# Output projection of a gated delta-rule block in float32 instead of float16 pairs

## The chip, the cores and the metric

The kernel runs on one core of one Trainium2 chip. The metric is the device time of one execution in microseconds; the median of three runs of the kernel before is 2579.32 us (2579.14 to 2581.09).

## The reference

The input x is 8 sequences of 512 tokens with 256 channels. Three sublayers are added to it in turn:

```
x = x + 0.5 * ffn(layernorm(x))
x = x + attention(layernorm(x))
x = x + 0.5 * ffn(layernorm(x))

attention(x):                      # 16 heads of 128 channels
  q, k, v = silu(conv4(x @ Wq)), silu(conv4(x @ Wk)) / sqrt(128), silu(conv4(x @ Wv))
  alpha, beta = sigmoid(x @ Wa + ba), sigmoid(x @ Wb + bb)
  for each token:  S = alpha * S - beta * (S @ k - v) k^T ;  o = S @ q
  o = layernorm_per_head(o) * ln_w + ln_b
  o = o * sigmoid(x @ Wg)          # the gated rows
  return o @ Wo                    # the output projection: 2048 channels to 256
```

The change is in the last line of the attention. The feed-forward layers use weights rounded to 8-bit floats.

## The kernel before

The program has three phases: the first feed-forward layer, the attention, the second feed-forward layer. The residual stream stays in SBUF throughout.

The attention goes over 4 groups of 4 heads (`HG`, `U`), in each group over the 8 sequences, in each sequence over 4 chunks of 128 tokens: 128 steps. A step works on one chunk of 4 heads. There is no planner: each engine has a hand-written order of stages (its `step(s)`), in which stages of neighbouring chunks are interleaved, and semaphores between them. In step s TensorE (PE) projects chunk s+3, inverts the triangular system of chunks s and s+1 by six levels (`level_a`, `level_b`), updates the state with chunk s-1, and turns and projects the output rows of chunks s-1 and s-2.

Float32 products that should be nearly exact are in places done as three float16 products: each operand is split into a high and a low half, and high*high + low*high + high*low is added up in PSUM. The output projection is one of these places. For chunk t:

- ScalarE (ACT) `affine` (L1221) writes the normed rows, float32, to `oa`; GpSimd (POOL) `gated` (L937) multiplies them with the gate.
- ACT `high` (L1229) writes the float16 high half `oh`; POOL `low` (L944) writes the low half `ol`.
- PE `output` (L1476) does 4 heads x 3 = 12 float16 matmuls, each with a stationary 128x128 tile of `oh` or `ol` and 256 moving columns of `wo16`.
- VectorE (DVE) `output` (L1060) adds the PSUM result, divided by 64, to the stream.

PE calls `output(s - 2)` in step s just before `level_b(s, 5)`, whose result ACT is waiting for.

The projection weights of a group are loaded in jobs (`load_job`, L1564 and L1567, on the SP queue) through four `raw` buffers; ACT (L1587, L1589) multiplies by 64 and writes the high half, POOL (L1597) the low half. A group has 16 jobs for Wk, Wq, Wv, Wg and 4 for Wo. For groups 1 to 3 they are done in the last steps of the group before (`JOB_STEPS`): the Wo jobs all in one step, on ACT and POOL in the same step in which PE first needs the new `wo16` (single-buffered, so no earlier). Group 0's jobs are spread over the first feed-forward layer.

Of the kernel before, what the change touches and what calls it, by code (L numbers as in the profile page):

```python
# [8 lines left out]
F16 = mybir.dt.float16  # L9
# [22 lines left out]
CX = C + 1  # L32
JOBS = 4 * U + U
SLOTS = 4
WO_SLOTS = 1
JOB_STEPS = {0: (0, 1, 2), 1: (3, 4, 5), 2: (6, 7, 8), 3: (9, 10, 11), 4: (12, 13, 14), 5: (15,), 8: (16, 17, 18, 19)}
FIRST_JOB_STEP = -26
# [22 lines left out]
def ffn_phase(nc, first, x_in, y_out, stream, z16, kit, scratch, w):  # L60

    with ExitStack() as ctx:  # L62
# [84 lines left out]
        def _(sp):  # L147
# [26 lines left out]
            if first:  # L174
# [556 lines left out]
def attention_phase(nc, stream, z16, kit, scratch, w):  # L731

    with ExitStack() as ctx:
# [9 lines left out]
        def units(b):  # L743
# [4 lines left out]
        nhalf, epsd, minus, lnb, lnwn = (kit[k] for k in ("nhalf", "epsd", "minus", "lnb", "lnwn"))  # L748
        bcol, prm, kqv16, gate16, wo16 = (kit[k] for k in ("bcol", "prm", "kqv16", "gate16", "wo16"))

# [13 lines left out]
        on = sb("on", [P, U, D]); oa = sb("oa", [P, U, C])  # L764
        oh = sb("oh", [P, U, C], F16); ol = sb("ol", [P, U, C], F16)

# [4 lines left out]
            dve="scan at mix y0 y1 res w z bn mv out " + " ".join(f"{k}{j}" for k in ("tap", "conv") for j in range(U)),  # L771
            act="rhs16 w16 kdec t0 lev0 lev1 on oa oh "
                + " ".join(f"{k}{j}" for k in ("acc", "silu", "gate") for j in range(U)),
            pool="diag am tt al kg qg zs var rstd shift og ol",
        )
# [29 lines left out]
        def _(sp):  # L805
# [28 lines left out]
        def _(pool):  # L834
# [104 lines left out]

            def low(t):  # L940
                if not known(t):
                    return
# [8 lines left out]
            def step(s):  # L951
                root(s - 1)
                low(s - 2)
                system_low(s + 1)
# [14 lines left out]
        def _(dve):  # L969
# [144 lines left out]
        def _(act):  # L1114
# [101 lines left out]
            def affine(t):  # L1216
                if not known(t):
                    return
                act.wait_ge(m["pe_ot"], t + 1)
                need(act, m["pool_ol"], t)  # L1220
                nc.scalar.activation(oa[:, :, :], units(TURN), ACT.Identity, bias=lnb[:, :], scale=lnwn[:, :])\  # L1221
                    .then_inc(m["act_oa"], 1)

            def high(t):
                if not known(t):
                    return
                act.wait_ge(m["pool_og"], t + 1)
                need(act, m["pe_wo"], t)
                nc.scalar.activation(oh[:, :, :], oa[:, :, :], ACT.Copy).then_inc(m["act_oh"], 1)  # L1229

            def weights(s):
                for job in jobs_of(s):
                    group, x = divmod(job, JOBS)
                    if x < 4 * U:
                        need(act, m[f"pe_pj{x % U}"], NC * (B * group - 1) + x // U + 1)
                    else:
                        need(act, m["pe_wo"], NC * B * (group - WO_SLOTS + 1))
                    high_job(nc, kit, act, job)

            def step(s):  # L1240
# [12 lines left out]
                first_inverse(s + 1)  # L1253
                high(s - 2)
                acc(s + 3, 1)
# [17 lines left out]
        def _(pe):  # L1273
# [5 lines left out]
            def gram_k(t):  # L1279
# [7 lines left out]
                if t > 2:  # L1287
                    pe.wait_ge(m["act_oa"], t - 2)
                else:
                    need(pe, m["dve_mix"], t)  # L1290
                    need(pe, m["act_kdec"], nk(t))
                cols = slice(c * C, (c + 1) * C)
# [4 lines left out]
            def gram_q(t):  # L1297
# [7 lines left out]
                pe.wait_ge(m["dve_at"], t + 1)  # L1305
                cols = slice(c * C, (c + 1) * C)
# [4 lines left out]
            def k_turned(t):  # L1311
                if not known(t) or t % NC == NC - 1:
                    return
                n, c = divmod(t, NC)
                pe.wait_ge(m["dve_mix"], t + 1)
                for u in range(U):
# [64 lines left out]
            def first_solution(t):  # L1381
# [4 lines left out]
                pe.wait_ge(m[f"act_lev{par}"], NL * (t // 2 + 1))  # L1386
                if t > 1:
                    pe.wait_ge(m["dve_out"], t - 1)
                else:
                    need(pe, m["dve_w"], t)  # L1390
                    need(pe, m["dve_z"], nk(t))
                for u in range(U):
# [53 lines left out]
            def out_turned(t):  # L1446
# [3 lines left out]
                if known(t + 2) and (t + 2) % NC < NC - 1:  # L1450
                    pe.wait_ge(m["act_kdec"], nk(t + 2) + 1)
                elif known(t + 2):
                    pe.wait_ge(m["dve_mix"], t + 3)
                else:
                    pe.wait_ge(m["act_oa"], t)
                for u in range(U):
# [3 lines left out]
            def output(t):  # L1460
# [4 lines left out]
                if n % B == 0 and c == 0:  # L1465
                    pe.wait_ge(kit["pool_wl"], JOBS * (group + 1))
                pe.wait_ge(m["pool_ol"], t + 1)
                if known(t + 1) and (t + 1) % NC < NC - 1:
                    pe.wait_ge(m["dve_z"], nk(t + 1) + 1)
                elif known(t + 1):  # L1470
                    pe.wait_ge(m["dve_w"], t + 2)
                else:
                    pe.wait_ge(m["dve_out"], t)
# [81 lines left out]
def load_job(nc, kit, w, sp, job):  # L1555
# [5 lines left out]
    need(sp, kit["pool_wl"], job - SLOTS + 1)  # L1561
    if x < 4 * U:
        src = w[("Wk", "Wq", "Wv", "Wg")[x // U]].rearrange("(k p) (h d) -> h p k d", p=P, d=D)[h]
        sp.dma_start(kit["raw"][:, slot].rearrange("p (k d) -> p k d", k=KT), src).then_inc(kit[f"dma_w{slot}"], 16)  # L1564
    else:
        src = w["Wo"].rearrange("(h p) n -> h p n", p=P)[h]
        sp.dma_start(kit["raw"][:, slot], src).then_inc(kit[f"dma_w{slot}"], 16)  # L1567


def split_of(kit, job, which):  # L1570
# [3 lines left out]
    if i < 3:  # L1574
        return kit["kqv16"][:, which, i, j].rearrange("p k d -> p (k d)")
    if i == 3:
        return kit["gate16"][:, which, j].rearrange("p k d -> p (k d)")
    return kit["wo16"][:, group % WO_SLOTS, which, j]

# [21 lines left out]
def macaron(nc, names, aps, out):  # L1601
# [5 lines left out]
    with ExitStack() as ctx:  # L1607
        stream = ctx.enter_context(nc.sbuf_tensor("stream", [P, B, TT, H], F32))
        with ExitStack() as inner:
            def sb(name, shape, dt=F32):  # L1610
# [9 lines left out]
                raw=sb("raw", [P, SLOTS, H]), kqv16=sb("kqv16", [P, 2, 3, U, KT, D], F16),  # L1620
                gate16=sb("gate16", [P, 2, U, KT, D], F16), wo16=sb("wo16", [P, WO_SLOTS, 2, U, H], F16))
            for k in [f"dma_w{i}" for i in range(SLOTS)] + ["act_w64", "act_wh", "pool_wl"]:
                kit[k] = inner.enter_context(nc.semaphore("k_" + k))
# [25 lines left out]
```

## Time and profile before

| | |
|---|---|
| median of 3 runs | 2579.32 us |
| profiled execution, its own time | 2582.29 us |
| its span | 2580.1 us |
| mean granted TensorE clock | 0.978 |
| PE busy | 2401.2 us, 93% |
| ACT / DVE / POOL busy | 78% / 77% / 64% |

The table is from one profiled execution; its span runs from the first to the last instruction. PE is TensorE's matmuls, PEld its weight loads, which run beside them. Matmuls are pipelined: one takes longer from its start to its end than the distance to the next one's start, and the distance is what it costs. So costs are read as (start of the next group - start of this group) / count. A float32 matmul is two matmul instructions in the trace (four heads of 128x128 stand there as x8), a float32 transpose one.

### The profile page before, as it was taken

Reading aid. Unit: us, or ns where it says so; the run is one execution under the profiler, and the core shown is the slowest. Engines: PE = TensorE matmul, PEld = TensorE weight load, DVE = VectorE, ACT = ScalarE, POOL = GpSimd, SP = SyncE. Lnnn points to the kernel's source line nnn. Section 1 sums busy time; section 2 is a strip of 40 time slices with the busy share of each in tenths; the row PEclk is TensorE's granted clock in tenths of the full one; section 3 lists DMA queues with packets and bytes.
Section 4 is the critical chain, followed back from the end, with each engine's and each line's share of the span. In section 5 each row is a group of like instructions: output and inputs, shape, how many; then the busy total and the mean of one; then the engine's idle time right before and its main releaser. Section 6 shows DMA issues by size and latency. Waiting matters only on the chain. (4 is left out here: it accounts for less than half of the span.)

```text
span 2580.1 us, 64359 instructions
## 1 busy us (share of the span) xinstructions
PE 2401.2 (93%) x24496; PEld 1838.1 (71%) x24496; DVE 1993.1 (77%) x4217; ACT 2018.4 (78%) x3848; POOL 1659.0 (64%) x1929
## 2 busy tenths in 40 slices
PE   4996899999999999999999999999999999999598
PEld 2553677777777777777777777777777777777365
DVE  5555888888878788888788888888778888887254
ACT  2884788888888788888887888888888888887364
POOL 7662566666677666666676666667766666666365
PEclk8998999999999999999999999999999999999799
DMA  5000111111121011111111111111111111111001
GB/s 137 22 14 8 34 30 28 27 29 31 36 55 40 23 30 30 30 31 30 47 42 38 31 30 31 29 27 40 50 38 30 29 27 28 29 31 28 23 26 41
DMA packets 80610, 87.86 MB, mean 34 GB/s; under 512 B 21937, under 2 KB 50609, under 8 KB 80177
## 3 DMA queue, kind: packets, MB, share of 16 engines
q1 hardware_dynamic: 80304, 83.75, 12.5%
q8 instruction: 196, 3.21, 0.5%
q14 instruction: 110, 0.89, 0.1%
HBM read 77.83 MB, written 5.90 MB: 32 GB/s over the span
## 5 line engine op out<-in xcount | busy, mean ns | idle before, releaser
L1496 PE MATMUL a_bank<-k_z,k_kqv 128*128 128x512 f16 x2304 | 588.8, 380 | 11.9 <-DVE a_kb L1073 5.9
L1187 ACT ACTIVATE a_inv<-a_bank 128x512 f16<-128x512 f32 x640 | 383.8, 605 | 123.2 <-PE a_bank L1354 122.8
L1004 DVE TENSOR_TENSOR k_y<-a_bank,k_masks 128x256 f16<-128x256 f32 x768 | 320.0, 420 | 176.8 <-PE a_bank L1340 169.1
L937 POOL TENSOR_TENSOR a_oa<-a_oa,a_gb 128x512 f32<-128x512 f32 x128 | 163.2, 1275 | 303.4 <-ACT a_oa L1221 303.4
L859 POOL TENSOR_TENSOR a_am<-a_at,k_ident 128x512 f16<-128x512 f32 x128 | 162.9, 1273 | 241.1 <-DVE a_at L989 241.1
L1496 PEld LDWEIGHTS a_bank<-k_z,k_kqv 128*128 128x128 f16 x2304 | 200.9, 98 | 155.4 <-issue 17.8
L1340 PEld LDWEIGHTS a_bank<-a_inv,a_am 128*128 128x128 f16 x3072 | 164.8, 98 | 198.3 <-ACT a_inv L1187 80.9
L1073 DVE SCALAR_TENSOR_TENSOR a_kb<-a_bank,k_prm,a_kb 128x511 f32<-128x511 f32 (+2 forms) x384 | 281.0, 739 | 19.1 <-ACT a_kb L1131 15.2
L1073 DVE SCALAR_TENSOR_TENSOR a_vb<-a_bank,k_prm,a_vb 128x511 f32<-128x511 f32 (+2 forms) x384 | 280.9, 739 | 2.2 <-ACT a_vb L1131 0.6
L1073 DVE SCALAR_TENSOR_TENSOR a_qb<-a_bank,k_prm,a_qb 128x511 f32<-128x511 f32 (+2 forms) x384 | 280.6, 738 | 1.8 <-ACT a_qb L1131 1.5
L1354 PE MATMUL a_bank<-a_inv,k_y 128*128 128x64 f16 x3072 | 273.2, 193 | 0.4 <-DVE k_y L1004 0.4
L1340 PE MATMUL a_bank<-a_inv,a_am 128*128 128x64 f16 x3072 | 202.1, 194 | 53.6 <-ACT a_inv L1187 39.2
L1352 PE MATMUL a_bank<-k_y,a_inv 128*128 128x64 f16 x2560 | 237.5, 193 | 3.0 <-DVE k_y L1004 3.0
L1354 PEld LDWEIGHTS a_bank<-a_inv,k_y 128*128 128x128 f16 x3072 | 208.9, 98 | 20.3 <-DVE k_y L1004 0.5
L1352 PEld LDWEIGHTS a_bank<-k_y,a_inv 128*128 128x128 f16 x2560 | 199.6, 98 | 28.5 <-DVE k_y L1004 14.2
L1476 PE MATMUL a_bank<-k_wo,a_oh 128*128 128x256 f16 x1024 | 193.8, 277 | 20.8 <-POOL k_wo L1597 11.4
L1212 ACT ACTIVATE a_on<-a_bank,a_shift,a_rstd 128x128 f32<-128x128 f32 x512 | 193.0, 468 | 8.3 <-POOL a_shift L927 8.3
L1496 PE MATMUL a_bank<-k_z,k_gate 128*128 128x512 f16 x768 | 197.8, 382 | 0.3 <-DVE a_vb L1073 0.3
L1442 PE MATMUL a_bank<-a_wv,a_mix 128*128 128x128 f32 x1024 | 193.5, 281 | 0.2 <-DVE a_wv L1023 0.2
L905 POOL TENSOR_TENSOR a_qg<-a_qb,a_cum 128x512 f32<-128x512 f32 x96 | 113.1, 1178 | 96.1 <-PE a_bank L1442 96.1
L1441 PE MATMUL a_bank<-a_z,a_qg 128*128 128x128 f32 x768 | 164.7, 296 | 1.6 <-DVE a_wv L1023 1.6
L980 DVE TENSOR_TENSOR_SCAN a_prod<-a_decay,k_diag 128x516 f32<-128x516 f32 x128 | 157.9, 1233 | 1.1 <-ACT a_kdec L1162 1.1
(151 smaller groups left out, 6831.1 us busy)
## 6 DMA issues: line engine op xcount, KB each, us to landing
a_decay<-decay_rows SPq DMA_DIRECT2D x128, 258.0 KB, 3.3
a_cum<-cumulative_rows SPq DMA_DIRECT2D x96, 258.0 KB, 3.3
stream<-in_L_attn_x SPq DMA_DIRECT2D x8, 512.0 KB, 6.8
out<-stream SPq DMA_DIRECT2D x8, 512.0 KB, 2.9
k_raw<-in_L_attn_Wk SPq DMA_DIRECT2D x16, 128.0 KB, 3.6
k_raw<-in_L_attn_Wq SPq DMA_DIRECT2D x16, 128.0 KB, 3.4
k_raw<-in_L_attn_Wv SPq DMA_DIRECT2D x16, 128.0 KB, 2.9
k_raw<-in_L_attn_Wg SPq DMA_DIRECT2D x16, 128.0 KB, 3.5
```

Source lines behind the costliest of these rows:

```text
L937: nc.gpsimd.tensor_tensor(oa[:, :, :], oa[:, :, :], gb[:, n % 2, :, c * C:(c + 1) * C], ALU.mult).then_inc(m["pool_og"], 1)
L1004: nc.vector.tensor_tensor(even(y16[:, j], mb), bank[LEV[par]][:, 0:U * C // 2].rearrange("p (u b m) -> p u b m", u=U, m=mb), masks[:, j].r ...
L1073: nc.vector.scalar_tensor_tensor(out=dst[:, d:S], in0=bank[PJ[j % 2]][:, 0:S - d], scalar=prm[:, i, U * (n // B) + j, TAPS - 1 - d:TAPS - ...
L1187: nc.scalar.activation(both, bank[LEV[par]][:, :].rearrange("p (two b m) -> p two b m", two=2, m=mb), ACT.Copy).then_inc(m[f"act_lev{par}" ...
L1212: ins = nc.scalar.activation(on[:, u], bank[OUT][:, u * D:(u + 1) * D], ACT.Identity, bias=shift[:, u:u + 1], scale=rstd[:, u:u + 1])
L1340: mm = pe.matmul(at_half(LEV[par], 0, u), am16[:, par, u], halves(t16[par][:, u], mb, 0), start=True, stop=True)
L1352: pe.matmul(at_half(LEV[par], 0, u), tt16[par][:, u], halves(y16[:, j, u], mb, 0), start=True, stop=True)
L1354: mm = pe.matmul(at_half(LEV[par], half, u), y16[:, j, u], halves(tt16[par][:, u], mb, 1), start=True, stop=True)
L1441: pe.matmul(units(OUT)[:, u], qg[:, u], z[:, u], start=True, stop=False)
L1442: mm = pe.matmul(units(OUT)[:, u], mix[:, t % 2, u], wv[:, u], start=not c, stop=True)
L1476: mm = pe.matmul(bank[SUM][:, 0:H], o[:, u], wo16[:, group % WO_SLOTS, wh, u], start=(u == 0 and wh == 0 and o is oh), stop=(u == U - 1 an ...
L1496: mm = pe.matmul(bank[PJ[j % 2]][:, :], wt, z16[:, zh, k, cols], start=(x == 0), stop=(x == 5))
```

## The change

The output projection's operands stay float32: `oa` is the stationary operand and `wo`, loaded straight from DRAM, the moving one. ACT's `high` and POOL's `low` stages and the Wo jobs go. PE does 4 float32 matmuls a chunk. The rows' buffer `oa` is now read by PE, so `affine` waits for the projection of the chunk before. The four loads of Wo are issued by SP in the step in which the Wo jobs were loaded, behind a wait for the last product of the group before. Several of PE's waits are written anew with the same or already reached values.

```diff
-JOBS = 4 * U + U
+JOBS = 4 * U
-WO_SLOTS = 1
-JOB_STEPS = {0: (0, 1, 2), ..., 5: (15,), 8: (16, 17, 18, 19)}
+JOB_STEPS = {0: (0, 1, 2), ..., 5: (15,)}
+OUT_STEP = 8
...
+                load_out(nc, kit, w, sp, 0)                      # SP, first phase, after job 5
...
+                group, at_step = divmod(s + 1 + FIRST_JOB_STEP, NC * B)      # SP, step(s)
+                if at_step == OUT_STEP and 0 <= group < HG - 1:
+                    sp.wait_ge(m["pe_wo"], NC * B * (group + 1))
+                    load_out(nc, kit, w, sp, group + 1)
...
-            def low(t):                                          # POOL
-                pool.wait_ge(m["act_oh"], t + 1)
-                nc.gpsimd.tensor_tensor(ol[:, :, :], oa[:, :, :], oh[:, :, :],
-                                        ALU.subtract).then_inc(m["pool_ol"], 1)
...
-                nc.vector.scalar_tensor_tensor(out=x, in0=bank[SUM][:, 0:H], scalar=1.0 / WS, in1=x,
+                nc.vector.scalar_tensor_tensor(out=x, in0=bank[SUM][:, 0:H], scalar=1.0, in1=x,
...
                 act.wait_ge(m["pe_ot"], t + 1)                   # ACT, affine
-                need(act, m["pool_ol"], t)
+                need(act, m["pe_wo"], t)
-            def high(t):
-                act.wait_ge(m["pool_og"], t + 1)
-                need(act, m["pe_wo"], t)
-                nc.scalar.activation(oh[:, :, :], oa[:, :, :], ACT.Copy).then_inc(m["act_oh"], 1)
...
+                need(pe, m["act_w16"], t + 1)                    # PE, correction
+                need(pe, m["dve_w"], t + 1)                      # PE, update
...
-                    pe.wait_ge(kit["pool_wl"], JOBS * (group + 1))           # PE, output
-                pe.wait_ge(m["pool_ol"], t + 1)
+                    pe.wait_ge(kit["dma_wo"], 16 * U * (group + 1))
+                pe.wait_ge(m["pool_og"], t + 1)
...
-                for u in range(U):
-                    for wh, o in ((0, oh), (0, ol), (1, oh)):
-                        mm = pe.matmul(bank[SUM][:, 0:H], o[:, u], wo16[:, group % WO_SLOTS, wh, u],
-                                       start=(u == 0 and wh == 0 and o is oh), stop=(u == U - 1 and wh == 1))
+                for u in range(U):
+                    mm = pe.matmul(bank[SUM][:, 0:H], oa[:, u], wo[:, u], start=(u == 0), stop=(u == U - 1))
...
+def load_out(nc, kit, w, sp, group):
+    for j in range(U):
+        src = w["Wo"].rearrange("(h p) n -> h p n", p=P)[U * group + j]
+        sp.dma_start(kit["wo"][:, j], src).then_inc(kit["dma_wo"], 16)
```

## Rows read from the trace of the kernel before

**Rows 1.** The page's first part: busy us (share of the span) xinstructions.
```profile
PE 2401.2 (93%) x24496; PEld 1838.1 (71%) x24496; DVE 1993.1 (77%) x4217; ACT 2018.4 (78%) x3848; POOL 1659.0 (64%) x1929
```
**Rows 2.** Busy time by window: PE, PEld, DVE, ACT, POOL, clock, DMA share, GB/s.
```profile
770.78:836.56 65.78, 64.48 (x708) 51.20 (x709) 55.99 (x119) 57.00 (x113) 46.35 (x53) 1.00 0.15 40
836.56:908.08 71.52, 66.35 (x708) 52.01 (x709) 56.03 (x119) 57.12 (x113) 45.47 (x53) 0.98 0.10 28
...
1911.63:1983.20 71.57, 66.42 (x708) 52.16 (x709) 56.02 (x119) 57.10 (x113) 45.45 (x53) 0.98 0.10 28
```
**Rows 3.** Waits of PE, whole span: us in total, times, longest.
```profile
PE a_bank L1340 <- ACT a_inv L1187: 39.2, 70, 2.7
```
**Rows 4.** PE in order of time: start, us, instruction, [idle before <- releaser].
```profile
811.72 0.29 PE L1340 MATMUL a_bank<-a_inv,a_am 128*128 128x64 f16 x4 [0.20 <-ACT a_inv L1187]
...
836.56 0.29 PE L1340 MATMUL a_bank<-a_inv,a_am 128*128 128x64 f16 x4 [0.71 <-ACT a_inv L1187]
...
850.37 0.39 PE L1476 MATMUL a_bank<-k_wo,a_oh 128*128 128x256 f16 x1 [3.79 <-POOL k_wo L1597]
```
**Rows 5.** PE in order of time, parts of one step without idle time.
```profile
1300.27 1.06 PE L1377 MATMUL a_bank<-a_z,a_kg 128*128 128x128 f32 x8
1301.16 0.19 PE L1352 MATMUL a_bank<-k_y,a_inv 128*128 128x64 f16 x1
...
1301.40 0.27 PE L1476 MATMUL a_bank<-k_wo,a_oh 128*128 128x256 f16 x1
...
1302.71 0.28 PE L1354 MATMUL a_bank<-a_inv,k_y 128*128 128x64 f16 x4
...
1314.22 1.14 PE L1308 MATMUL a_bank<-a_qb,a_kb 128*128 128x128 f32 x8
1315.19 0.19 PE L1352 MATMUL a_bank<-k_y,a_inv 128*128 128x64 f16 x1
...
1315.43 1.46 PE L1496 MATMUL a_bank<-k_z,k_kqv 128*128 128x512 f16 x6
1316.72 0.40 PE L1340 MATMUL a_bank<-a_inv,a_am 128*128 128x64 f16 x8
```
**Rows 6.** PE in the first phase: float32 matmuls with 32 moving columns.
```profile
98.39 1.07 PE L677 MATMUL f_bank<-f_ident,f_ab 32*128 32x32 f32 x8
99.39 0.28 PE L652 MATMUL f_bank<-f_wq,f_hh 128*128 128x256 f16 x1
```
**Rows 7.** ACT in order of time, around the idle times of rows 4.
```profile
808.16 0.62 ACT L1229 ACTIVATE a_oh<-a_oa 128x512 f16<-128x512 f32 x1
808.79 1.28 ACT L1151 ACT_TABLE_LOAD   x1
...
1303.02 0.38 ACT L1181 ACTIVATE a_inv<-a_bank 128x256 f16<-128x256 f32 x1 [0.32 <-PE a_bank L1354]
```
**Rows 8.** SP's DMA issues, and the page's row on their landing.
```profile
832.48 1.86 SPq L1567 DMA_DIRECT2D k_raw<-in_L_attn_Wo  x4
```
```profile
k_raw<-in_L_attn_Wo SPq DMA_DIRECT2D x16, 128.0 KB, 3.6
```
**Rows 9.** First phase: a Wo job on ACT, and PE's next wait.
```profile
179.29 0.41 ACT L1587 ACTIVATE k_raw<-k_raw 128x256 f32<-128x256 f32 x1
...
182.17 1.10 PE L606 MATMUL f_bank<-f_ident,f_ztok 128*128 128x128 f32 x8 [1.02 <-ACT f_ztok L497]
```
**Rows 10.** All engines at the end of the attention, in order of time.
```profile
2398.70 0.28 PE L1476 MATMUL a_bank<-k_wo,a_oh 128*128 128x256 f16 x1 [1.01 <-POOL a_ol L944]
...
2409.93 1.51 ACT L1212 ACTIVATE a_on<-a_bank,a_shift,a_rstd 128x128 f32<-128x128 f32 x4 [6.34 <-POOL a_shift L927]
...
2413.59 1.06 PE L1457 MATMUL a_bank<-k_ident,a_on 128*128 128x128 f32 x4
...
2415.54 1.26 POOL L937 TENSOR_TENSOR a_oa<-a_oa,a_gb 128x512 f32<-128x512 f32 x1 [4.54 <-ACT a_oa L1221]
...
2418.75 0.39 PE L1476 MATMUL a_bank<-k_wo,a_oh 128*128 128x256 f16 x1 [4.10 <-POOL a_ol L944]
```

More of the change, by code:

```diff
@@ L32 @@
 CX = C + 1
-JOBS = 4 * U + U
+JOBS = 4 * U
 SLOTS = 4
-WO_SLOTS = 1
-JOB_STEPS = {0: (0, 1, 2), 1: (3, 4, 5), 2: (6, 7, 8), 3: (9, 10, 11), 4: (12, 13, 14), 5: (15,), 8: (16, 17, 18, 19)}
+JOB_STEPS = {0: (0, 1, 2), 1: (3, 4, 5), 2: (6, 7, 8), 3: (9, 10, 11), 4: (12, 13, 14), 5: (15,)}
+OUT_STEP = 8
 FIRST_JOB_STEP = -26
@@ L748, in attention_phase @@
         nhalf, epsd, minus, lnb, lnwn = (kit[k] for k in ("nhalf", "epsd", "minus", "lnb", "lnwn"))
-        bcol, prm, kqv16, gate16, wo16 = (kit[k] for k in ("bcol", "prm", "kqv16", "gate16", "wo16"))
+        bcol, prm, kqv16, gate16, wo = (kit[k] for k in ("bcol", "prm", "kqv16", "gate16", "wo"))
         qb = sb("qb", [P, 2, U, S]); kb = sb("kb", [P, 2, U, S]); vb = sb("vb", [P, 2, U, S])
@@ L764, in attention_phase @@
         on = sb("on", [P, U, D]); oa = sb("oa", [P, U, C])
-        oh = sb("oh", [P, U, C], F16); ol = sb("ol", [P, U, C], F16)
         tiles = [f"{k}{j}" for k in ("pj", "acc", "tap", "conv", "silu", "gate") for j in range(U)]
@@ L771, in attention_phase @@
             dve="scan at mix y0 y1 res w z bn mv out " + " ".join(f"{k}{j}" for k in ("tap", "conv") for j in range(U)),
-            act="rhs16 w16 kdec t0 lev0 lev1 on oa oh "
+            act="rhs16 w16 kdec t0 lev0 lev1 on oa "
                 + " ".join(f"{k}{j}" for k in ("acc", "silu", "gate") for j in range(U)),
-            pool="diag am tt al kg qg zs var rstd shift og ol",
+            pool="diag am tt al kg qg zs var rstd shift og",
         )
@@ L952, in step @@
                 root(s - 1)
-                low(s - 2)
                 system_low(s + 1)
@@ L1233, in weights @@
                     group, x = divmod(job, JOBS)
[L1234 to L1237, printed above, removed]
+                    need(act, m[f"pe_pj{x % U}"], NC * (B * group - 1) + x // U + 1)
                     high_job(nc, kit, act, job)
@@ L1253, in step @@
                 first_inverse(s + 1)
-                high(s - 2)
                 acc(s + 3, 1)
@@ L1286, in gram_k @@
                         pe.wait_ge(m[f"act_silu{j}"], 3 * n + 1)
-                if t > 2:
-                    pe.wait_ge(m["act_oa"], t - 2)
-                else:
-                    need(pe, m["dve_mix"], t)
-                    need(pe, m["act_kdec"], nk(t))
+                if known(t - 3):
+                    need(pe, m["act_oa"], t - 2)
+                elif known(t - 1) and (t - 1) % NC < NC - 1:
+                    need(pe, m["act_kdec"], nk(t - 1) + 1)
+                elif known(t - 1):
+                    need(pe, m["dve_mix"], t)
+                else:
+                    need(pe, m["dve_at"], t)
                 cols = slice(c * C, (c + 1) * C)
@@ L1304, in gram_q @@
                         pe.wait_ge(m[f"act_silu{j}"], 3 * n + 2)
-                pe.wait_ge(m["dve_at"], t + 1)
+                need(pe, m["dve_at"], t + 1)
                 cols = slice(c * C, (c + 1) * C)
@@ L1314, in k_turned @@
                 n, c = divmod(t, NC)
-                pe.wait_ge(m["dve_mix"], t + 1)
+                need(pe, m["dve_mix"], t + 1)
                 for u in range(U):
@@ L1386, in first_solution @@
                 pe.wait_ge(m[f"act_lev{par}"], NL * (t // 2 + 1))
-                if t > 1:
-                    pe.wait_ge(m["dve_out"], t - 1)
-                else:
-                    need(pe, m["dve_w"], t)
-                    need(pe, m["dve_z"], nk(t))
+                if known(t - 2):
+                    need(pe, m["dve_out"], t - 1)
+                elif known(t - 1) and (t - 1) % NC < NC - 1:
+                    need(pe, m["dve_z"], nk(t - 1) + 1)
+                elif known(t - 1):
+                    need(pe, m["dve_w"], t)
+                else:
+                    need(pe, m["act_w16"], t)
                 for u in range(U):
@@ L1450, in out_turned @@
                 if known(t + 2) and (t + 2) % NC < NC - 1:
-                    pe.wait_ge(m["act_kdec"], nk(t + 2) + 1)
+                    need(pe, m["act_kdec"], nk(t + 2) + 1)
                 elif known(t + 2):
-                    pe.wait_ge(m["dve_mix"], t + 3)
+                    need(pe, m["dve_mix"], t + 3)
+                elif known(t + 2):
+                    need(pe, m["dve_at"], t + 3)
                 else:
-                    pe.wait_ge(m["act_oa"], t)
+                    need(pe, m["act_oa"], t)
                 for u in range(U):
@@ L1465, in output @@
                 if n % B == 0 and c == 0:
-                    pe.wait_ge(kit["pool_wl"], JOBS * (group + 1))
-                pe.wait_ge(m["pool_ol"], t + 1)
+                    pe.wait_ge(kit["dma_wo"], 16 * U * (group + 1))
+                pe.wait_ge(m["pool_og"], t + 1)
                 if known(t + 1) and (t + 1) % NC < NC - 1:
-                    pe.wait_ge(m["dve_z"], nk(t + 1) + 1)
+                    need(pe, m["dve_z"], nk(t + 1) + 1)
                 elif known(t + 1):
-                    pe.wait_ge(m["dve_w"], t + 2)
+                    need(pe, m["dve_w"], t + 2)
+                elif known(t + 1):
+                    need(pe, m["act_w16"], t + 2)
                 else:
-                    pe.wait_ge(m["dve_out"], t)
+                    need(pe, m["dve_out"], t)
                 for u in range(U):
-                    for wh, o in ((0, oh), (0, ol), (1, oh)):
-                        mm = pe.matmul(bank[SUM][:, 0:H], o[:, u], wo16[:, group % WO_SLOTS, wh, u],
-                                       start=(u == 0 and wh == 0 and o is oh), stop=(u == U - 1 and wh == 1))
+                    mm = pe.matmul(bank[SUM][:, 0:H], oa[:, u], wo[:, u], start=(u == 0), stop=(u == U - 1))
                 mm.then_inc(m["pe_wo"], 1)
@@ L1561, in load_job @@
     need(sp, kit["pool_wl"], job - SLOTS + 1)
[L1562 to L1567, printed above, removed]
+    src = w[("Wk", "Wq", "Wv", "Wg")[x // U]].rearrange("(k p) (h d) -> h p k d", p=P, d=D)[h]
+    sp.dma_start(kit["raw"][:, slot].rearrange("p (k d) -> p k d", k=KT), src).then_inc(kit[f"dma_w{slot}"], 16)
+def load_out(nc, kit, w, sp, group):
+    for j in range(U):
+        src = w["Wo"].rearrange("(h p) n -> h p n", p=P)[U * group + j]
+        sp.dma_start(kit["wo"][:, j], src).then_inc(kit["dma_wo"], 16)
 def split_of(kit, job, which):
@@ L1575, in split_of @@
         return kit["kqv16"][:, which, i, j].rearrange("p k d -> p (k d)")
-    if i == 3:
-        return kit["gate16"][:, which, j].rearrange("p k d -> p (k d)")
-    return kit["wo16"][:, group % WO_SLOTS, which, j]
+    return kit["gate16"][:, which, j].rearrange("p k d -> p (k d)")
 def high_job(nc, kit, act, job):
@@ L1620, in macaron @@
                 raw=sb("raw", [P, SLOTS, H]), kqv16=sb("kqv16", [P, 2, 3, U, KT, D], F16),
-                gate16=sb("gate16", [P, 2, U, KT, D], F16), wo16=sb("wo16", [P, WO_SLOTS, 2, U, H], F16))
-            for k in [f"dma_w{i}" for i in range(SLOTS)] + ["act_w64", "act_wh", "pool_wl"]:
+                gate16=sb("gate16", [P, 2, U, KT, D], F16), wo=sb("wo", [P, U, H]))
+            for k in [f"dma_w{i}" for i in range(SLOTS)] + ["dma_wo", "act_w64", "act_wh", "pool_wl"]:
                 kit[k] = inner.enter_context(nc.semaphore("k_" + k))
```

4 lines of the change are left out of this document (removed).

## The prediction

> **What bounds the kernel now.** I read the page's busy shares first, then busy time by window, then PE's waits, then PE, ACT and POOL in order of time over two steps. PE is the busiest engine by share [rows 1], but a share is no proof. The windows are: four steps in the middle of the attention take 65.78 us, of which PE is busy 64.48 at the full clock, while ACT has 57.00, DVE 55.99 and POOL 46.35 [rows 2]. The 1.3 us that PE lacks are three short waits for ACT in four steps, two of which are shown: 0.20 and 0.71 us [rows 4]; over the span waits of this kind come to 39.2 us [rows 3]. Between them PE's groups start the moment the group before is through: the float32 group that starts at 1300.27, the output projection at 1301.40 and the level behind it at 1302.71 have no idle time before them [rows 5]. So in the 128 steps a microsecond added to PE's stream is a microsecond of the kernel, and work taken from ACT or POOL is worth only what PE waits for it.
>
> **PE's part.** The 12 float16 matmuls of one chunk go from 1301.40 to 1302.71: 1.31 us, 0.109 each for 256 columns [rows 5]. In their place come 4 float32 matmuls of 256 columns, 8 instructions. The trace has no float32 instruction of 256 columns, so its distance is bounded. At 128 columns it is (1301.16 - 1300.27) / 8 = 0.111 us [rows 5], the same as a float16 instruction of twice as many columns. That can have two reasons: each float32 column takes two of a float16 column's slots, or the float32 weight load takes 0.11 us and hides the stream. By the first, 256 columns cost what 512 float16 columns do, 1.29 / 6 = 0.215 [rows 5], or at most twice 0.111 = 0.222. By the second, they stay at 0.111. The float32 instructions with 32 columns speak for some floor by the load: 1.00 / 8 = 0.125 us each, although they stream a quarter of the columns [rows 6]. But a floor and a stream of two slots a column fit together at 128 columns, where both give 0.11. I take 0.218, twice the 0.109 of a float16 instruction with 256 columns.
>
> The Trainium skill, FP8 and Floating Point Precision, section TensorE Precision Notes, says that true float32 takes four passes through the array, high and low halves crossed. Two instructions a matmul in the trace leave two passes for each, which is the first reading; 0.111 at 128 columns agrees with it, and no row here shows it at 256. By that page alone the stage would be 16 passes of 0.109, the same 1.74 us.
>
> A float32 group that follows 64-column float16 matmuls can't hide its first weight load: the group at 1314.22 takes 0.97 us where the one at 1300.27 takes 0.89 [rows 5], so 0.08 more (between 0 and 0.11). The new stage follows such matmuls too. It takes 8 x 0.218 + 0.08 = 1.82 us, 0.51 more than now (0.41 to 0.58). 126 of the 128 chunks are projected with PE's stream on the path: +64.3 us (+52 to +73). None of it is covered: PE's two waits of rows 4 come behind ACT work that starts from `level_b(s, 5)`, which PE does after the output projection. ACT has been waiting 0.32 us for it [rows 7], so ACT shifts with PE and the waits stay as long. DVE's add, the scan behind it and SP's decay load behind the scan start from the same point and shift as well.
>
> The rewritten waits of PE ask for values already reached; the two added ones (`correction`, `update`) repeat what the engine has seen, in stages that follow the one before without a gap. I take 0, and at most 0.02 us a step, 2.5 us in all; below 0 nothing can come of them.
>
> **ACT's and POOL's part.** `high` is 0.62 us a chunk [rows 7]; it goes, and `low` with it. POOL waits for others at all its stages and is not the last releaser of any PE wait in mid-attention: nothing gained or lost there. ACT's `high` stands directly ahead of a table load (808.16, 808.79) in a run of ACT work without a gap that ends in PE's wait of 0.20 us at 811.72 [rows 4, 7]. So this wait goes, once in four steps, some 31 times: -6.3 us (0 to -7). The wait of 0.71 stays: `high` is not in its run, which begins at the ACT instruction of 1303.02 [rows 7].
>
> **The Wo jobs.** At 850.37 PE has waited 3.79 us for POOL's last Wo split, and starts at half the clock [rows 4]: ACT's and POOL's eight and four instructions are all in the step in which PE needs them. The four steps with this wait take 71.52 and 71.57 us in the first and last of three cases, 65.78 without [rows 2]: 5.76 x 3 = -17.3 us, of which 3.8 is the wait and the rest the low clock behind it and what ACT has late. In its place stands a wait for a DMA. SP issued the old Wo loads at 832.48 [rows 8]; the new wait on SP (the last product of the old group) is met by then, since SP has first waited in the same step for a DVE scan that DVE does after adding that product. Queued behind it on SP are the next cumulative and decay rows, so it would matter; it is free. Landing takes 3.6 us [rows 8], so the weights are there some 8 us before PE needs them at 846.6. If that is wrong, a part of the 17.3 comes back.
>
> In the first feed-forward layer four jobs go. A job's two ACT instructions of some 0.4 us each (the first at 179.29) stand ahead of the norm that PE waits 1.02 us for at 182.17 [rows 9]. This happens at two sequences: -1.6 us (0 to -2). SP's four new loads are issued in a gap in which it waits for POOL.
>
> **The end of the attention.** PE is no longer full, and the chain runs through the last chunks. The wait of 1.01 us for `ol` at 2398.70 goes. The last transposes start at 2413.59 because the projection before them waited for `ol`; without that they start when ACT's norm ends, 2409.93 + 1.51 = 2411.4: -2.1. From the end of the last gating, 2415.54 + 1.26 = 2416.8, to the last projection at 2418.75 there are 1.9 us of `high` and `low`, which go. The last projection itself runs at half the clock and is 0.9 longer, one before it 0.5 [rows 10]. Sum: -3.6 us (-2 to -5).
>
> **The sum.** 64.3 - 6.3 - 17.3 - 1.6 - 3.6 = +35.5 us on the profiled execution's 2582.3, so 2617.8 there. That execution is 3.0 us above the median, a constant for this purpose: the prediction for the median is 2579.3 + 35.5 = 2615 us. With the ends of the terms: 2599 to 2628.
>
> **Rivals.**
>
> A. The load sets the pace, not the columns. An instruction of 256 float32 columns then costs what one of 128 does, 0.111 us, and the stage 8 x 0.111 + 0.08 = 0.97 us, 0.34 less than now: -43 - 29 = -72, 2507 us. For it speaks that 32 columns cost as much as 128 [rows 6]; against it that 0.111 is so exactly twice the float16 distance of 128 columns. The Trainium skill, TensorE: Matmul & The Clock Gate, sections LDWEIGHTS and Weight-path perf modes, gives a load as columns / 1.2 ns and says that float32 has no fast one; 107 ns for 128 columns is close to the 0.111 us here, and by that rule alone this rival holds. Chance 0.08.
>
> B. PE's waits take up what is added. They are 1.3 us in four steps; if all were room, 40 us of the 64 would vanish: 2579 - 4 = 2575 us. Against it: the order of stages, as worked out above. Chance 0.03.
>
> C. The load is not hidden under a longer stream: 0.218 + 0.111 = 0.329 an instruction, 2.7 us a stage, +1.4 x 126 = +177 - 29, so 2727 us. Against it: at 128 columns loads and streams overlap fully [rows 5]. Chance 0.02.
>
> D. The gain at the group borders does not come, because the new DMA wait or a later clock drop takes its place: +53, 2632 us. Chance 0.04.
>
> **How the numbers follow.** The forecast has 0.83. A measurement of this kernel tells 0.2%, 5 us, from no change. Faster: A and half of B, 0.09. Same: the rest of B and a little of an unforeseen mix of terms, 0.03. Slower: the forecast, C, D, 0.88. The range 2600 to 2630 is the forecast's own, 2599 to 2628, moved up a little towards D; it leaves out A, B and C.
>
> **What would show it.** In the changed profile a float32 group at the output projection's line, x8, with some 1.8 us to the next group (A: 1.0; C: 2.7) and 0.21 to 0.22 between its instructions. Four steps at 67.6 us instead of 65.8 with a wait of 0.71 left and that of 0.20 gone. No PE wait for weights at the three group borders. PE's busy time up, ACT's down by 128 x 0.62 = 79 us for `high` and 16 x 0.8 = 13 for the jobs, POOL's down as well. I am wrong if the stage's length is not near 1.8, or if four steps do not grow by four times what the stage grows.

## The result and the profile after

The kernel with the change takes 2598.55 us (median of 4 runs, 2596.09 to 2600.65), the kernel before 2580.20 us beside it (4 runs, 2579.14 to 2581.91). The ratio is 1.0069 with a 95% interval of 1.0054 to 1.0084: 18 us slower. The forecast was +35.5. The profiled execution of after has a span of 2595.7 us, that of before 2580.1, so +15.6.

The first part of the page of after, which answers to [rows 1]:

```profile
PE 2446.1 (94%) x23984; PEld 1878.8 (72%) x23984; DVE 1993.3 (77%) x4217; ACT 1948.7 (75%) x3688; POOL 1499.0 (58%) x1785
```

PE is busy 45 us longer, ACT 70 and POOL 160 us less. By window, one steady stretch of four steps and one that holds a group border (both run from one PE wait of 0.71 us to the next, called a cycle below); they answer to [rows 2], with one difference: the cycle of 65.78 us shown there holds two steps of weight jobs. A cycle of before without any (1446.37 to 1512.16) takes as long, but with ACT at 54.66 us in 105 instructions and POOL at 42.95 in 49, and these are the numbers to compare with:

```profile
366.98:434.12 67.14, 66.15 (x693) 52.69 (x693) 56.03 (x119) 52.80 (x101) 38.53 (x45) 1.00 0.12 29
843.10:910.25 67.15, 66.16 (x692) 52.69 (x693) 56.02 (x119) 52.81 (x101) 38.56 (x45) 1.00 0.10 30
```

A steady cycle is 1.36 us longer than the 65.78 of before, and the border cycle is no longer than the steady one: the 5.7 us that a border cost are gone. PE's waits of [rows 3] shrink from 39.2 to 33.5 us and from 70 to 43:

```profile
PE a_bank L1328 <- ACT a_inv L1183: 33.5, 43, 2.5
```

The projection's stage, PE in order of time, between the same neighbours as in [rows 5]:

```profile
1309.29 0.19 PE L1342 MATMUL a_bank<-a_inv,k_y 128*128 128x64 f16 x1
1309.32 1.97 PE L1472 MATMUL a_bank<-k_wo,a_oa 128*128 128x256 f32 x8
1311.13 0.28 PE L1342 MATMUL a_bank<-a_inv,k_y 128*128 128x64 f16 x4
```

It takes 1311.13 - 1309.32 = 1.81 us, where 12 float16 instructions took 1.31. Read the distance of the starts, not the 1.97, which overlaps the next group.

SP issues the weights of the next group in the step before PE needs them, and PE's first use of them at the border has no idle time before it (where [rows 4] had 3.79 us):

```profile
839.02 1.86 SPq L1565 DMA_DIRECT2D k_wo<-in_L_attn_Wo  x4
```
```profile
852.72 1.97 PE L1472 MATMUL a_bank<-k_wo,a_oa 128*128 128x256 f32 x8
```

The second row starts 13.7 us after the first, and the page gives a landing of 3.1 us.

### The profile page after: what moved, and what is told of

Same layout as the page of the kernel before. It is cut to its first block and busy times, and to the rows that moved or that the text cites. A ratio compares the mean times of both kernels' runs of the same rounds, so it can differ in the third digit from the quotient of the medians.

```text
span 2595.7 us, 63017 instructions
## 1 busy us (share of the span) xinstructions
PE 2446.1 (94%) x23984; PEld 1878.8 (72%) x23984; DVE 1993.3 (77%) x4217; ACT 1948.7 (75%) x3688; POOL 1499.0 (58%) x1785
## 5 line engine op out<-in xcount | busy, mean ns | idle before, releaser
L1472 PE MATMUL a_bank<-k_wo,a_oa 128*128 128x256 f32 x1024 | 253.9, 391 | 2.2 <-POOL a_oa L941 2.2
L1328 PE MATMUL a_bank<-a_inv,a_am 128*128 128x64 f16 x3072 | 201.0, 193 | 43.0 <-ACT a_inv L1183 33.5
L1342 PEld LDWEIGHTS a_bank<-a_inv,k_y 128*128 128x128 f16 x3072 | 208.4, 98 | 35.5 <-issue 0.5
L1472 PEld LDWEIGHTS a_bank<-k_wo,a_oa 128*128 128x128 f32 x1024 | 185.4, 191 | 22.6 <-POOL a_oa L941 2.4
L1056 DVE SCALAR_TENSOR_TENSOR stream<-a_bank,stream 128x256 f32<-128x256 f32 x128 | 54.4, 425 | 155.1 <-PE a_bank L1472 155.1
```

What stands on the lines that cost most here:

```text
L1328: mm = pe.matmul(at_half(LEV[par], 0, u), am16[:, par, u], halves(t16[par][:, u], mb, 0), start=True, stop=True)
L1342: mm = pe.matmul(at_half(LEV[par], half, u), y16[:, j, u], halves(tt16[par][:, u], mb, 1), start=True, stop=True)
L1472: mm = pe.matmul(bank[SUM][:, 0:H], oa[:, u], wo[:, u], start=(u == 0), stop=(u == U - 1))
```

## Where the forecast was off: the gate step

In one step of four ACT has the gate's work to do, with a table load before the silu of `v` (L1141 before) and another before the gate (L1151); it is called the gate step here. The same stretch of PE in both kernels, from the 0.28 us wait to the transposes behind the second `level_a`. First before:

```profile
808.32 0.29 PE L1340 MATMUL a_bank<-a_inv,a_am 128*128 128x64 f16 x4 [0.28 <-ACT a_inv L1170]
...
809.66 1.46 PE L1496 MATMUL a_bank<-k_z,k_gate 128*128 128x512 f16 x6
811.23 0.29 PE L1340 MATMUL a_bank<-a_inv,a_am 128*128 128x64 f16 x4
...
811.85 0.63 PE L1317 MATMUL a_bank<-k_ident,a_kb 128*128 128x128 f32 x4
```

and after:

```profile
814.49 0.29 PE L1328 MATMUL a_bank<-a_inv,a_am 128*128 128x64 f16 x4 [0.28 <-ACT a_inv L1166]
...
815.83 1.46 PE L1491 MATMUL a_bank<-k_z,k_gate 128*128 128x512 f16 x6
817.12 0.55 PE L1328 MATMUL a_bank<-a_inv,a_am 128*128 128x64 f16 x8
817.51 0.63 PE L1305 MATMUL a_bank<-k_ident,a_kb 128*128 128x128 f32 x4
```

From the first row to the transposes: 3.53 us before, 3.02 after. That is 0.51 us, where the list of waits had named only 0.20 [rows 4]. The other part stands in no bracket. The six projection instructions take 817.12 - 815.83 = 1.29 us when nothing holds the next group, and took 811.23 - 809.66 = 1.57 before: 0.28 us of waiting that no row mentions. The rest, 0.62 against 0.39 from the first `level_a` group to the transposes, is the 0.20 that is listed and 0.03 more. The reason is in the durations: 1.46 us is printed for six instructions that hold the next one up for 1.29. A group's modelled end lies 0.17 us behind the moment from which PE could go on, so a bracket shows a wait that much too short. Of the 0.28 us the view is left with 811.23 - (809.66 + 1.46) = 0.11, and it prints no bracket for so little.

ACT in the same step of after, against 808.16 and 808.79 of [rows 7]:

```profile
813.85 0.58 ACT L1166 ACTIVATE a_inv<-a_bank 128x512 f16<-128x512 f32 x1
814.45 1.28 ACT L1147 ACT_TABLE_LOAD   x1
```

The table load now follows the instruction ahead of the old copy by 0.60 us. Before, that instruction (L1170) started at 807.68 and the load at 808.79: 1.11. ACT's gap-free run is shorter by 0.51, and PE, which waits for its end, gets all of it.

## The experiments

Two theories stood behind the first two runs: the missing gain is the ACT copy `high`, worth more than its listed wait; or it is POOL's `low`, which the forecast had priced at nothing.

**e1_high_back**: the kernel after, with the copy in its old place; nobody reads what it writes.

```diff
+            def high(t):
...
+                act.wait_ge(m["pool_og"], t + 1)
+                nc.scalar.activation(oh[:, :, :], oa[:, :, :], ACT.Copy)
...
                 first_inverse(s + 1)
+                high(s - 2)
```

> The changed kernel with ACT's `high` put back in its old place (an ACT copy of `oa` to a float16 tile that nobody reads; nobody waits for it). Theory 1: in one step of four ACT is one run without a gap from the gate's table load to the system's first solution, and PE lost the whole length of `high`, some 0.6 us, to it, of which the view of waits showed 0.20. Put back, four steps grow by 0.51 us from 67.14 to 67.65 (0.1 of the 0.6 is covered by the longer output stage), so +14 to +20 us over the changed kernel, about +16. Theory 2 (as predicted before): only the wait of 0.20 us hangs on `high`: +6 us, four steps 67.34. Theory 3: the 14 us missing in the sum have nothing to do with ACT (clock, waits rewritten): 0.

Measured: 2612.64 us (4 runs), ratio to before 1.0136 (1.0120 to 1.0153), where after had 1.0069: about 17 us for the copy alone (11 to 23 by the two intervals). PE's waits in one cycle:

```profile
1394.22 0.29 PE L1336 MATMUL a_bank<-a_inv,a_am 128*128 128x64 f16 x4 [0.71 <-ACT a_inv L1184]
1432.76 0.29 PE L1336 MATMUL a_bank<-a_inv,a_am 128*128 128x64 f16 x4 [0.28 <-ACT a_inv L1167]
1436.15 0.29 PE L1336 MATMUL a_bank<-a_inv,a_am 128*128 128x64 f16 x4 [0.20 <-ACT a_inv L1184]
1461.88 0.29 PE L1336 MATMUL a_bank<-a_inv,a_am 128*128 128x64 f16 x4 [0.71 <-ACT a_inv L1184]
```

The cycle is 67.66 us, 0.51 over that of after, and the listed wait of 0.20 is back. ACT is busy 2014.8 us, 66 over after, which is 0.52 a copy: of its 0.62 us the first 0.1 lies under the end of the instruction before it.

**e2_low_back**: the kernel after, with POOL's subtraction in its old place and ACT's `affine` waiting for it; nobody reads the result.

```diff
+            def low(t):
...
+                pool.wait_ge(m["pool_og"], t + 1)
+                nc.gpsimd.tensor_tensor(ol[:, :, :], oa[:, :, :], oa[:, :, :],
+                                        ALU.subtract).then_inc(m["pool_ol"], 1)
```

> The changed kernel with POOL's `low` put back in its old place (a subtraction of the same size from `oa` into a float16 tile that nobody reads; ACT's `affine` waits for it as before the change). Theory 1 and 2: POOL is nobody's last releaser in mid-attention, four steps stay at 67.14 us and the time within 3 us of the changed kernel. Rival: part of what ACT seemed to give came from POOL's 148 us: four steps at 67.3 or more, +5 us or more.

Measured: 2600.14 us (5 runs), ratio 1.0089 (1.0074 to 1.0105), overlapping the interval of after. The cycle:

```profile
1386.67:1453.82 67.15, 66.16 (x693) 52.69 (x693) 56.01 (x119) 52.80 (x101) 42.49 (x49) 1.00 0.11 30
```

POOL does 4 us more in it and it stays at 67.15. The theory of `low` falls for the steady steps.

**e3_cols64 and e4_cols128**: the kernel after with the output projection on 64 and on 128 of the 256 columns.

```diff
-                x = stream[:, n % B, c]
-                nc.vector.scalar_tensor_tensor(out=x, in0=bank[SUM][:, 0:H], scalar=1.0, in1=x,
+                x = stream[:, n % B, c, 0:64]
+                nc.vector.scalar_tensor_tensor(out=x, in0=bank[SUM][:, 0:64], scalar=1.0, in1=x,
...
-                    mm = pe.matmul(bank[SUM][:, 0:H], oa[:, u], wo[:, u], start=(u == 0), stop=(u == U - 1))
+                    mm = pe.matmul(bank[SUM][:, 0:64], oa[:, u], wo[:, u, 0:64], start=(u == 0), stop=(u == U - 1))
```

> The changed kernel with 64 moving columns in place of 256 in the output projection (three quarters of its output columns are left out). If a float32 instruction has a floor set by its weight load: 8 x 0.111 + 0.08 = 0.97 us a stage. If it costs two slots a column and the load is no floor: 8 x 0.056 = 0.45 us. PE shorter by 0.84 (or 1.36) us a step; how much of it the kernel gives back shows how near the other engines are: by PE alone -105 (or -170) us.

> The changed kernel with 128 moving columns in the output projection (half of its output columns are left out). Both readings: 8 x 0.111 + 0.08 = 0.97 us a stage, 0.84 less than with 256. Beside the run with 64 columns: the same stage length if the load is the floor, twice it if not. The kernel: -105 us if PE alone bounds it, less where ACT's runs do.

Measured, in one run each: 2501.55 us with 64 columns and 2510.26 with 128. The stage and the group behind it, with 64 and with 128:

```profile
1441.48 1.08 PE L1472 MATMUL a_bank<-k_wo,a_oa 128*128 128x64 f32 x8
1442.39 0.28 PE L1342 MATMUL a_bank<-a_inv,k_y 128*128 128x64 f16 x4
```
```profile
1448.16 1.14 PE L1472 MATMUL a_bank<-k_wo,a_oa 128*128 128x128 f32 x8
1449.13 0.28 PE L1342 MATMUL a_bank<-a_inv,k_y 128*128 128x64 f16 x4
```

0.91 and 0.97 us, against 1.81 with 256. So half of 128 columns saves only 0.06 us over 8 instructions, and twice as many cost 0.84. Inside both short groups the instructions start 0.11 us apart, and inside the long one 0.216. Both readings that the prediction weighed are true, each in its place: up to 128 columns there is a floor of about 0.11 us an instruction, above it a float32 column takes two slots. The cycles are 64.12 and 64.24 us, so taking 4 x 0.84 = 3.36 us of PE work out of a cycle shortens it by 67.14 - 64.24 = 2.90. The missing 0.46 lies in the gate step, where PE now comes too early. With 128 columns `first_solution` (L1384) starts 1386.36 - 1384.90 = 1.46 us after the `level_b` group behind the projection:

```profile
1384.90 0.28 PE L1342 MATMUL a_bank<-a_inv,k_y 128*128 128x64 f16 x4
1385.16 0.63 PE L1452 MATMUL a_bank<-k_ident,a_on 128*128 128x128 f32 x4
...
1386.36 0.38 PE L1384 MATMUL a_bank<-a_rhs,a_inv 128*128 128x128 f16 x4
```

In after it is 1430.03 - 1429.01 = 1.02. In the short version both stages start just behind ACT: the transposes wait for its `kdec`, which ends at 1385.02, and `first_solution` for its `inv`, which ends at 1386.27. Here ACT's run holds PE, and a microsecond of PE is no longer a microsecond of the kernel. In time that is 88 us less than after where PE alone would have given 105; with one run each, and the stretch before the first cycle 299.8 us in after and 305.4 with 128 columns, the cycles are the better measure.

The next two leave the product alone and change the kernel before, one removed cost each.

**e7_high_on_pool**: POOL writes the float16 half itself, as a second product ahead of the float32 one; ACT's copy goes.

```diff
+                nc.gpsimd.tensor_tensor(oh[:, :, :], oa[:, :, :], gb[:, n % 2, :, c * C:(c + 1) * C],
+                                        ALU.mult).then_inc(m["pool_oh"], 1)
+                pool.wait_ge(m["pool_oh"], t + 1)
                 nc.gpsimd.tensor_tensor(oa[:, :, :], oa[:, :, :], gb[:, n % 2, :, c * C:(c + 1) * C],
...
-                high(s - 2)
```

> The kernel before with one edit: the float16 high half is written by POOL (a second product of rows and gate, straight to float16, some 1.3 us) in place of ACT's copy. Nothing changes in PE's work. Theory 1: ACT's run in one step of four is 0.6 us shorter, PE gets back 0.63 us in four steps (65.79 to 65.16), -18 to -20 us; POOL has the room (46 of 66 us busy). Theory 2: only the wait of 0.20 goes: -6 us. Rival: POOL's added 1.3 us, which stands ahead of the system's split that PE's first inverse waits for, costs as much or more: 0 or slower.

**e5_wo_jobs_early**: POOL does its part of the Wo jobs in the step before, behind `first_inverse`.

```diff
-                weights(s)
+                weights(s, False)
                 gated(s - 1)
                 system16(s + 2)
                 first_inverse(s + 2)
+                weights(s + 1, True)
```

> The kernel before with one edit: POOL does the four Wo jobs of a group before `scaled_q` at the end of its step, where it waits for PE, instead of behind `root` in the next step. It isolates the term of the group borders. Theory: PE's wait of 3.79 us for the last split and the half clock behind it go, 4 to 5.8 us at each of three borders: -12 to -17 us from the kernel before, 2564 to 2568. Rival: the jobs only move the lateness to ACT's norm, which then waits for POOL's `root`, and PE waits there instead: less than -6 us.

Measured: e7 2565.39 us (5 runs), ratio 0.9944 (0.9932 to 0.9957), or -14.4 us; e5 2566.02 us (5 runs), ratio 0.9951 (0.9937 to 0.9965), or -12.6. A steady cycle of e7 and the border cycle of e5:

```profile
1434.44:1499.69 65.25, 64.26 (x708) 51.26 (x708) 55.97 (x119) 52.52 (x101) 48.03 (x53) 1.00 0.12 30
```
```profile
837.23:903.82 66.59, 64.83 (x709) 50.89 (x709) 55.83 (x119) 57.07 (x113) 45.75 (x53) 1.00 0.11 30
```

With the copy off ACT the cycle shrinks by 0.53 us, 31.5 x 0.53 = 16.7, although POOL does more. The expected 0.63 and -18 to -20 us were too much; the end of the attention, from the last wait of 0.71 us at the start of a cycle to the last addition on DVE, also took 2.1 us longer (111.9 against 109.8), and the added product on POOL lies in that chain. The border cycle is 66.59 us instead of 71.52: 4.9 of the 5.7 us come back by a change of order alone, and a wait of 0.38 us for DVE is new. Neither needs a float32 product.

**e6_both**: both edits in the kernel before.

> The kernel before with both edits of the two other kernels of this set: POOL does the Wo jobs early and writes the high half. The float16 products stay. If the terms add up: -17 - 19 = -36 us, 2544 us, faster than both the kernel before and the changed one. If POOL becomes the bound at the borders: -25 or less.

Measured: 2551.70 us (4 runs, 2549.89 to 2554.36), ratio 0.9894 (0.9881 to 0.9908). That is faster than both kernels. The gain is 27 us by the ratio, and the two single ones are 14.4 + 12.6 = 27.0, so they add up; the 36 expected was too much because each alone had been. Steady cycle:

```profile
1425.03:1490.30 65.27, 64.28 (x709) 51.29 (x709) 55.98 (x119) 52.53 (x101) 48.01 (x53) 1.00 0.12 30
```

**e8_product_alone**: the kernel before with the float32 product and nothing else, except that `affine` waits for the projection as in after. The float32 weights are the bits of the float16 pairs, so sizes and order are those of the change and the values are not. This splits the sum of the prediction in two.

```diff
-                    for wh, o in ((0, oh), (0, ol), (1, oh)):
-                        mm = pe.matmul(bank[SUM][:, 0:H], o[:, u], wo16[:, group % WO_SLOTS, wh, u],
...
+                wide = wo16[:, :, :, :, :].rearrange("p s w u h -> p (s w u h)").bitcast(F32)
...
+                    mm = pe.matmul(bank[SUM][:, 0:H], oa[:, u], wide[:, H * u:H * (u + 1)], start=(u == 0), stop=(u == U - 1))
```

> The kernel before with one part of the change alone: the projection multiplies the float32 rows by float32 weights (8 instructions in place of 12). The copy of the high half, the subtraction of the low half, the Wo jobs and their waits all stay as before. The weights are the bits of the float16 pairs read as float32, so the projection's values are not the reference's; sizes and order are. Theory 1 (the stage's growth of 0.50 us is not quite uncovered; the run with the high copy put back showed 67.65 per four steps): four steps at 67.6 to 67.7, +1.86 over the kernel before, with waits of about 0.20 and 0.71 left; border waits of 3.8 us and cycles of about 73.4 there. In time 31.5 x 1.86 = +59, between +55 and +63 with the tail, so some 2637 us. Theory 2 (the prediction's sum: nothing of it is covered): four steps at 67.8, +64 us, 2644 us. If the time is below 2630, something in the start or in the tail, not the cycles, gives back what the cycles add.

Measured: 2644.83 us (5 runs), ratio 1.0261 (1.0246 to 1.0275). A steady cycle and a border cycle:

```profile
924.42:992.08 67.66, 66.36 (x692) 52.60 (x693) 56.02 (x119) 54.82 (x105) 42.96 (x49) 1.00 0.12 29
1403.82:1477.36 73.54, 68.38 (x693) 53.71 (x693) 56.01 (x119) 57.27 (x113) 45.47 (x53) 0.98 0.11 27
```

By the cycle theory 1 is right (67.66, not 67.8). By the time it looks like theory 2: +66.6, with an interval from +63 to +71. The two profiles differ by 62.1, because the profiled execution of before, with 2582.29 us, lies 4.0 above the median of 2578.25 beside these runs, and that of e8 lies 1.0 below its own. The time is more than the 31.5 x 1.87 = 59 of theory 1 because of two stretches that are no steady cycles; they stand below.

The profiled executions, cut at the first and the last PE wait of 0.71 us that starts a cycle (a later one, among the last chunks, is not counted) and at the end of the last projection's addition on DVE:

| us | before | product alone | after | product: measured (forecast) | the rest: measured (forecast) |
|---|---|---|---|---|---|
| start to the first mark | 305.64 | 303.25 | 299.83 | -2.4 (0) | -3.4 (-1.6) |
| 30 cycles | 2006.51 | 2065.44 | 2031.68 | +58.9 (+61.2) | -33.8 (-23.3) |
| last mark to the last addition | 109.79 | 114.74 | 105.91 | +5.0 (+4.5) | -8.8 (-5.3) |
| second feed-forward layer | 158.15 | 158.71 | 158.26 | +0.6 (0) | -0.5 (0) |
| span | 2580.1 | 2642.2 | 2595.7 | +62.1 (+65.7) | -46.5 (-30.2) |

The forecasts are those of the prediction, shared out: 120 of its 126 stages, 30 of its waits and the three borders lie in the cycles, the rest of them in the stretch behind, with the 0.9 + 0.5 us for half the clock there under the product. The -2.4 of the first line is not the product's doing, which has hardly begun there: between 255 and 275 us the granted clock was 0.91 in the execution of before and 1.00 in the other two, some 1.8 us. Nor does the first line show the -3.4 to be the rest's: four kernels with the first phase of after (e1 to e4) have 302.0, 301.8, 301.9 and 305.4 us there.

Three of the 30 cycles are long in every kernel: the ones in which four steps of the other weight jobs run. In the first of them in before ACT waits for a weight load, does three jobs and only then turns to the gate step, and PE waits 2.27 us for it:

```profile
733.88 0.42 ACT L1587 ACTIVATE k_raw<-k_raw 128x256 f32<-128x256 f32 x1 [1.16 <-DMA k_raw<-in_L_attn_Wq]
...
738.71 0.29 PE L1340 MATMUL a_bank<-a_inv,a_am 128*128 128x64 f16 x4 [2.27 <-ACT a_inv L1187]
```

These cycles take 3.7 to 6.9 us more than a steady one, in sum 15.4 us in before, 17.9 in the product alone, 17.3 in after, 15.6 in e1 and 13.8 in e6. So 2.5 of the 58.9 us are theirs, as much as the executions differ here anyway, and the change takes nothing from them. No run moved these jobs, though in all they cost nearly as much as the Wo jobs did.

## Why the prediction was right or wrong

The direction, the sign of the balance and most terms were right. The time came out 16 us under the forecast and just under the range. The range itself was added up wrongly: with the ends of the terms as they stand it is 2600 to 2635.5, not 2599 to 2628.

1. **PE's part: right in mechanism, a little too large.** The stage was forecast at 1.82 us and takes 1.81, 0.216 an instruction and 0.08 for the exposed first load. The Trainium skill, FP8 and Floating Point Precision, section TensorE Precision Notes, says four passes for float32. Two passes in each of the two instructions, twice the 0.109 of float16, agree with the 0.216. Rival C is refuted. Rival A fails at 256 columns, and its floor exists at 64 and 128. The prediction read 0.125 at 32 columns from [rows 6], but that is an average up to the next group's start; inside that group the instructions start 0.112 apart, the same floor. The Trainium skill, TensorE: Matmul & The Clock Gate, section LDWEIGHTS, gives a load as columns / 1.2 ns, an estimate of 107 ns for 128 columns of weights. The runs with 64 and 128 columns agree at 0.11. Taken as the pace at 256 columns too, that load would make the stage some 0.9 us by the same estimate, and the measured 1.81 denies it.
   "None of it is covered" was nearly true: a cycle grows by 1.87 us in e8, not by 4 x 0.50 = 2.0. The 0.13 lies in the gate step. Behind the projection `first_solution` came 815.44 - 814.30 = 1.14 us after the `level_b` group in before, and comes 1382.18 - 1381.17 = 1.01 after it in e8 (821.47 - 820.46 in after). In before it waited a little for ACT, below what the view prints, and a later PE no longer does; with the shorter stage of e4 the same distance is 1.46. Over 31.5 cycles the 0.13 is 4 us, and the 0.01 of the stage is 1 more.

2. **"So this wait goes, once in four steps, some 31 times: -6.3 us": this is the step that failed.** The place and the run of ACT work were right and the size was not. The copy is worth 0.51 us a cycle (e1: 67.66 against 67.15; e7: 0.53), 31.5 x 0.51 = 16 us. The forecast took the listed wait as all that PE lost and gave the term an end of -7, but the copy's own time on ACT, in a run without a gap that ends in a wait of PE, was the bound to keep: 128 x 0.62 is not it, 31.5 x 0.5 is. Ten of the missing 16 to 20 microseconds (16 by the medians, 20 by the profiles) are here, and with this bound the range would have reached down to some 2590. By the table the other parts are the start (4.2 in both columns together, where the executions differ by as much without a cause in the change), the end of the attention (3, see 5) and the product in the cycles (2.3).

3. **POOL's `low`: nothing gained or lost in the steady steps.** Right (e2). Not quite so at the end, see 5.

4. **The Wo jobs: right.** e8 has 73.54 at a border and after 67.15; with the steady cycles at 67.66 the three borders are worth 3 x 5.88 = 17.6 us, where 17.3 was forecast. The DMA wait on SP is free, the weights land some 9 us before PE's first use (the four are issued until 840.88, landing takes 3.1, the use is at 852.72), and rival D is refuted. e5 shows that the cost was mostly the order of POOL's work. In the first feed-forward layer PE's wait of 1.02 us at 182.17 [rows 9] is now 0.27:

```profile
179.68 1.09 PE L607 MATMUL f_bank<-f_ident,f_ztok 128*128 128x128 f32 x8 [0.27 <-ACT f_ztok L498]
```

   That agrees with the 0.8 us a sequence of the forecast: the wait is 0.26 to 0.27 in all five kernels without these jobs and 1.02 in all five with them. Another 1.7 us came between there and the next wait at this line (40.51 us before, 38.84 after), and it is not the jobs' doing: e5, e7 and e8 still do them and have 38.8, and e6 has 40.5. The granted clock of that stretch was 0.87 in before, 0.86 in e6 and 0.94 in after, e5, e7 and e8.

5. **The end of the attention: the gain was forecast too small.** Together the product and the rest were to take 0.8 us off this stretch, and 3.9 went. The chain of after, all engines in order of time:

```profile
2425.42 1.89 PE L1472 MATMUL a_bank<-k_wo,a_oa 128*128 128x256 f32 x8
...
2430.31 0.66 PE L1452 MATMUL a_bank<-k_ident,a_on 128*128 128x128 f32 x4 [3.00 <-ACT a_on L1208]
...
2431.86 1.26 POOL L941 TENSOR_TENSOR a_oa<-a_oa,a_gb 128x512 f32<-128x512 f32 x1 [3.14 <-ACT a_oa L1217]
...
2433.18 3.78 PE L1472 MATMUL a_bank<-k_wo,a_oa 128*128 128x256 f32 x8 [2.21 <-POOL a_oa L941]
```

   and of the product alone:

```profile
2470.46 3.78 PE L1476 MATMUL a_bank<-k_wo,a_oa 128*128 128x256 f32 x8 [4.29 <-POOL a_ol L944]
...
2474.04 1.06 PE L1457 MATMUL a_bank<-k_ident,a_on 128*128 128x128 f32 x4
...
2479.20 3.78 PE L1476 MATMUL a_bank<-k_wo,a_oa 128*128 128x256 f32 x8 [4.10 <-POOL a_ol L944]
```

   The waits for `ol` go, as forecast, and the transposes no longer stand behind a projection that waits. The row that the forecast did not have is the first: without the wait of 4.29 us ahead of it, the last projection but one runs at the full clock (granted 1.00, where the product alone has 0.50, which is 2.4 and 1.2 GHz): 1.89 us instead of 3.78. The last one waits 2.21 us and again runs at 0.50. With `high` put back the stretch is 109.7 us and with `low` 107.4, against 105.9, so the copy is worth 3.8 us here (0.8 of them are the 1.5 cycles that the 31.5 of point 2 count too) and the subtraction 1.5, in one execution each.

6. **Rival B** (PE's waits take up what is added, 0.03) had no part in it: both remaining waits of a cycle, 0.28 and 0.71, are as long as before. What gave back more was not PE's slack but ACT's run.

The prediction's own tests: the stage near 1.8, yes; no wait for weights at the borders, yes; four steps at 67.6, no, 67.14; ACT's busy time down by 79 + 13, no, by 70. Of these 66 are the copy (e1), since an instruction's duration overlaps its neighbour's by a tenth of a microsecond and busy time counts the overlap once; that leaves 4 for the jobs instead of 13, and no run takes this apart.

## What to carry to other kernels

Where work is taken off an engine that runs without a gap into a wait of the bounding engine, price it by that engine's distances between starts, with and without the instruction, and take this as one end of the range; the listed wait is only the other end. (Here 1.11 us with the copy and 0.60 without, and a listed wait of 0.20.) When a change trades one resource for several others, look whether the gains need the trade: here the copy's place and the order of the weight jobs could be had without the float32 product, and the kernel that does so is 1.1% faster than the one before and 1.7% faster than the one after (1.0069 against 0.9894).

## What the hardware showed that was not expected

- A float32 matmul instruction with 128 columns of weights costs 0.11 us with 64 or 128 moving columns and 0.216 with 256, so narrowing below 128 columns gains next to nothing.
- PE's idle time is counted from a modelled end 0.17 us behind the stream. In the gate step it showed 0.20 us of a loss of 0.51.
- During a wait of 4.29 us PE's granted clock fell to 0.50, and the next projection took 3.78 us; without that wait the same group took 1.89 at 1.00.
- ACT instructions in a row overlap by 0.1 us: the copy's 0.62 cost 0.51 between starts.
